# Causal attention with a gate, then eight routed experts, on one Trainium2 core: the start, the hand-over to the first expert and the last products put in another order, and one pair of batches fewer by one-hot products

## What is computed

```python
# x [16,128,256], ctx [16,128,256]; 8 experts, 512 slots each, token numbers drawn with repeats
x = x + xattn(layernorm(x), ctx)      # keys: rmsnorm(x) (causal) beside ctx, softmax, gate by sigmoid
...
h = layernorm(x).reshape(-1, 256)     # 2048 token rows
gathered = h[top_idx.T]               # [8, 512, 256]
g = gelu(gathered @ W1 + b1)          # [8, 512, 1024]
out_e = g @ W2 + b2
out = zeros.at[tok].add(out_e * combine_weights[tok, e])
return x + out
```

## Time and profile before

| | |
|---|---|
| median of 3 runs | 277.23 us (276.16 to 277.33) |
| the profiled execution: time | 277.63 us |
| the profiled execution: span from first to last instruction | 275.8 us |
| around the span | 1.8 us |
| mean granted TensorE clock | 0.991 |
| busy: PE, DVE, ACT, POOL | 265.7, 219.0, 188.2, 155.9 us |
| HBM read, written | 33.54 MB, 9.24 MB |

### The profile page before, as it was taken

The page is one execution under the profiler, slowest core; times in us unless marked ns, Lnnn a source line. Parts: engine busy times, 40 slices in busy tenths (PEclk is TensorE's granted clock), DMA queues, the critical chain, the costliest instruction groups (busy, mean ns, idle before and its releaser), DMA issues.

```text
span 275.8 us, 5127 instructions
## 1 busy us (share of the span) xinstructions
PE 265.7 (96%) x1474; PEld 226.7 (82%) x1474; DVE 219.0 (79%) x554; ACT 188.2 (68%) x349; POOL 155.9 (57%) x153
## 2 busy tenths in 40 slices
PE   6999999999989999999999999999999999999992
PEld 2688899999866888888888888888888888888992
DVE  1788999898986499968878896796887889689452
ACT  2488898887575976685677587658657758763540
POOL 4283865655843956556446466655645646605515
PEclk9799999999999999999999999999999999999998
DMA  7993247568454956455565544546555461201211
GB/s 219 358 263 94 77 123 218 155 214 276 114 182 123 350 160 157 124 192 167 138 195 163 154 139 135 157 122 209 156 138 189 156 175 53 67 26 47 62 38 69
DMA packets 30292, 42.44 MB, mean 154 GB/s; under 512 B 5251, under 2 KB 24015, under 8 KB 30148
## 3 DMA queue, kind: packets, MB, share of 16 engines
q1 hardware_dynamic: 25392, 30.00, 34.4%
q0 software_dynamic: 4608, 12.24, 15.4%
q10 hardware_dynamic: 276, 0.00, 0.1%
HBM read 33.54 MB, written 9.24 MB: 155 GB/s over the span
## 4 chain that ended last, share of the span: by engine, by line
PE 83%; DVE 6%; issue 4%; POOL 3%; ACT 2%; DMA 1%; DVEq 0%; POOLq 0%; ACTq 0%
PE bank L1398 19%; PE bank L1185 13%; PE bank L1186 12%; PE bank L1187 12%; PE bank L1399 10%; PE bank L1229 4%; PE bank L1274 3%; PE bank L1326 2%; PE bank L1345 1%; PE bank L1349 1%; PE bank L1346 1%; DMA x_all<-in_x_dram 1%; PE bank L1181 1%; POOL out_dram L552 1%; PE bank L1258 1%
## 5 line engine op out<-in xcount | busy, mean ns | idle before, releaser
L742 ACT ACTIVATE keysT<-bank,biasT 128x512 f32<-128x512 f32 x63 | 43.7, 693 | 55.6 <-PE bank L1187 41.8
L552 POOL DMA_INDIRECT out_dram<-h,sidx x32 | 36.8, 1151 | 41.9 <-DVE h L1077 37.0
L543 POOL DMA_INDIRECT x_all<-out_dram,idx_all x32 | 35.4, 1106 | 23.9 <-DMA out_dram<-h,sidx 16.5
L1185 PE MATMUL bank<-x_hi,w_parts 128*128 128x512 f32 (+1 forms) x114 | 45.1, 396 | 0.0
L1186 PE MATMUL bank<-x_lo,w_parts 128*128 128x512 f32 (+1 forms) x114 | 44.4, 389 | 0.0
L1187 PE MATMUL bank<-x_hi,w_parts 128*128 128x512 f32 (+1 forms) x114 | 44.1, 387 | 0.0
L1102 DVE TENSOR_TENSOR g_lo<-keysT,g_hi 128x512 fp32r<-128x512 f32 x32 | 22.1, 690 | 24.9 <-ACT g_hi L743 23.4
L1398 PE MATMUL bank<-w_parts,g_hi 128*128 128x512 f32 x112 | 40.5, 396 | 0.0
L539 POOL DMA_INDIRECT x_all<-token_rows,idx_all x28 | 29.0, 1036 | 19.4 <-DVE factor L1126 7.7
L1107 DVE TENSOR_TENSOR w_parts<-w_raw,w_parts 128x512 fp32r<-128x512 f32 x56 | 38.9, 696 | 0.0
L748 ACT CAST w_parts<-w_raw 128x512 fp32r<-128x512 f32 x56 | 34.9, 623 | 0.0
(11 more groups left out here) (186 smaller groups left out, 685.9 us busy)
## 6 DMA issues: line engine op xcount, KB each, us to landing
w_raw<-in_L_ffn_W_dram SPq DMA_DIRECT2D x32, 512.0 KB
idx_rows<-in_L_ffn_top_idx_dram SPq DMA_DIRECT2D x8, 256.0 KB, 4.0
out_dram<-x SPq DMA_DIRECT2D x8, 256.0 KB, 3.0
hn_cnat<-in_ctx_dram SPq DMA_DIRECT2D x7, 256.0 KB, 2.7
token_rows<-xn SPq DMA_DIRECT2D x7, 256.0 KB, 2.2
hn_cnat<-in_L_ffn_b_dram SPq DMA_DIRECT2D x1, 1024.0 KB, 6.9
x_all<-in_x_dram SPq DMA_DIRECT2D x3, 256.0 KB, 4.4
x_all<-in_x_dram SPq DMA_DIRECT2D x1, 768.0 KB, 8.1
```

What stands on the lines that cost most here:

```text
L543: g.indirect_dma_start(accg[:, t, :], None, flat, list_of(e, t)).then_inc(acc_in[t], 16)
L552: g.indirect_dma_start(flat, idx(sidx[:, t:t + 1].bitcast(U32), 0), newrow[:, t, :], None, bounds_check=N - 1, oob_is_err=False).then_inc( ...
L742: a.activation(g32[:, f % NG, :], ps_up[f % 2][:, :], ACT.Gelu_apprx_tanh, bias=bias)
L1185: t_.matmul(dst, lhs_hi, rhs_hi, start=first, stop=False)
```

## The change

It does six things. The start: k_w's load goes to ACT's queue as its first, gate_b is loaded by partition like norm_w, the product with the row of ones is replaced by four transposes of broadcast columns, both halves of M come before the transposes of pair 0, the context of pair 0 is transposed before the queries, one more warm-up product is made, and DVE takes the statistics of batches 6 to 9 later. The pairs: `EARLY_PAIRS` is NPAIR - 2, so that pair 5 is stored and gathered and only pairs 6 and 7 go by one-hot products; all gathers of expert 0's first rows move into pair 7. Pairs 6 and 7: DVE takes the statistics of x2 ahead of the gate, POOL the rstd of pair 5 ahead of the weight piece. The masks come ahead of expert 1's gathers. The end: `last_downs` takes four steps, and the last scatters' waits stand on their own instructions. Cut to its core:

```diff
@@ -51 @@
     NG = 4
-    EARLY_PAIRS = NPAIR - 3
+    EARLY_PAIRS = NPAIR - 2
@@ -359 @@
     load_weight(0, q_w, wts_in)
-    load_weight(1, k_w, wts_in)
@@ -390 @@
             load_ctx(r + 3)
-        if r == EARLY_PAIRS - 2:
+        if r == EARLY_PAIRS - 3:
...
                 sp.dma_start(rows_v[:, 2 * r + b, 0:H], xn_last[:, b, :]).then_inc(xn_out[r % 2], 16)
+            sp.wait_ge(onehot_rdy, NB - EARLY)
+            load_lists(IDX_PARTS - 1)
@@ -405 @@
                 sp.wait_ge(first_rows_in[t], 16)
-            for late in (LAST - 2, LAST - 1):
-                sp.wait_ge(xn_rdy, 2 * late + 2)
-                sp.dma_start(rows_v[:, 2 * late:2 * late + 2, 0:H], xn2[:, late % 2, :, :])\
-                    .then_inc(xn_out[late % 2], 16)
-            sp.wait_ge(onehot_rdy, NB - EARLY)
-            load_lists(IDX_PARTS - 1)
+            sp.wait_ge(xn_rdy, 2 * r + 2)
+            sp.dma_start(rows_v[:, 2 * r:2 * r + 2, 0:H], xn2[:, r % 2, :, :]).then_inc(xn_out[r % 2], 16)
@@ -500 @@
         if is_last(p):
-            gather_first_rows(range(1, NT))
+            gather_first_rows(range(1))
@@ -511 @@
         else:
-            if not is_last(p):
+            if not stats_first(p):
...
             rstd(p - 1, 1 - s)
-        if p == LAST - 1:
-            gather_first_rows(range(1))
+            if p == LAST - 1:
+                expert0_lo(p - 1)
+        if is_last(p):
+            gather_first_rows(range(1, NT))
@@ -548 @@
             pool.wait_ge(new_rdy, NT * e + t + 1)
-            take_waits(pool)
+            if not is_last(e):
+                take_waits(pool)
...
-    for s in range(2):
-        pool.wait_ge(xn_out[s], 16 * (NPAIR // 2) + 16 + 16 * s)
-        pool.wait_ge(x2_out[s], 16 * (NPAIR // 2) + 16)
-    gather_rows(1, 1)
...
                         pattern=[[1, C]], channel_multiplier=-NT).then_inc(seen_rdy, 1)
+    for s in range(2):
+        pool.wait_ge(xn_out[s], 16 * (NPAIR // 2) + 16 + 16 * s)
+        pool.wait_ge(x2_out[s], 16 * (NPAIR // 2) + 16)
+    gather_rows(1, 1)
@@ -583 @@
     a = nc.scalar
-    act.dma_start(norm_wT[:, :], norm_w.rearrange("(k p) -> p k", p=P), allow_slow_non_contiguous=True)\
+    act.dma_start(wts[:, 1, :, :], k_w.rearrange("(k p) h -> p k h", p=P)).then_inc(wts_in, 16)
+    act.dma_start(norm_wT, norm_w.rearrange("(k p) -> p k", p=P), allow_slow_non_contiguous=True)\
         .then_inc(nwT_in, 16)
-    act.dma_start(vec_rows[:, 0:H], norm_w.rearrange("(a h) -> a h", a=1)).then_inc(vec_in, 16)
-    act.dma_start(vec_rows[:, H:2 * H], gate_b.rearrange("(a h) -> a h", a=1)).then_inc(vec_in, 16)
+    act.dma_start(norm_w_gate_bT[:, 1, :], gate_b.rearrange("(k p) -> p k", p=P),
+                  allow_slow_non_contiguous=True).then_inc(gate_b_in, 16)
@@ -642 @@
     def attention(p, s, use):
-        if is_last(p):
-            act.wait_ge(xn_rdy, 2 * p - 2)
-            act.wait_ge(q_mm, NPAIR)
-            a.copy(late_hi[0], xn2[:, s, :, :]).then_inc(late_hi_rdy, 1)
@@ -655 @@
             hn_transposed(p + 2, s)
+        if is_last(p):
+            expert0_hi(p)
+            act.wait_ge(setup_mm, 4)
+            a.copy(biasT[:, :], banks[0][:, 0:NE * NF]).then_inc(setup_ev, 1)
@@ -674 @@
                 act.wait_ge(w_in[c], 16)
-        expert0_hi(p)
-        if is_last(p):
...
-            act.wait_ge(setup_mm, 4)
-            a.copy(biasT[:, :], banks[0][:, 0:NE * NF]).then_inc(setup_ev, 1)
-            a.activation(table_junk[:, :], junk[:, 0:2], ACT.Gelu_apprx_tanh)
+        if not is_last(p):
+            expert0_hi(p)
@@ -689 @@
             act.wait_ge(xn_rdy, 2 * p)
-            a.copy(late_hi[1], xn2[:, 1 - s, :, :]).then_inc(late_hi_rdy, 1)
+            a.copy(late_hi[0], xn2[:, 1 - s, :, :]).then_inc(late_hi_rdy, 1)
+            a.activation(table_junk[:, :], junk[:, 0:2], ACT.Gelu_apprx_tanh)
     M_high(0)
+    M_high(1)
     hn_transposed(0, 0)
-    M_high(1)
+    context_transposed(0, 0)
...
     query(0)
-    context_transposed(0, 0)
@@ -841 @@
     M_low(0)
+    M_low(1)
+    hnT_low(0, 0)
     x_sums(3, 4, 1)
-    hnT_low(0, 0)
     x_aggregates(2, 4)
-    M_low(1)
...
     x_rms(0, 4, 2)
-    x_stats(6, 10, 3)
-    x_variances(6, 10)
+    x_sums(6, 8, 3)
@@ -921 @@
         if not is_first(p):
-            if not is_last(p):
+            if not isinstance(p, int):
...
             residual(p - 1, 1 - s, last_use)
+            if stats_first(p):
+                stats2(p - 1, 1 - s)
+                aggr2(p - 1, 1 - s)
...
             v.tensor_copy(idx_f[:, :], idx_all[:, :, :].rearrange("p t e -> p (t e)")).then_inc(idx_rdy, 1)
+            x_sums(8, 10, 3)
@@ -947 @@
         if is_first(p):
+            x_aggregates(6, 10)
+            x_variances(6, 10)
...
             x_stats(10, NB, 4)
-        else:
+        elif not stats_first(p):
...
         else:
-            aggr2(p - 1, 1 - s)
+            if stats_first(p):
+                shift(p - 1, 1 - s)
+            else:
+                aggr2(p - 1, 1 - s)
...
         v.reciprocal(rinv[:, :], rsum[:, :]).then_inc(ri_rdy, 1)
-        if is_last(p):
-            dve.wait_ge(late_hi_rdy, 1)
-            dve.wait_ge(xn_rdy, 2 * LAST - 2)
-            v.tensor_tensor(late_lo[0], xn2[:, s, :, :], late_hi[0].bitcast(F32), ALU.subtract)\
-                .then_inc(late_lo_rdy, 1)
...
             dve.wait_ge(x_steps, steps[0])
-        elif not is_last(p):
+        elif not stats_first(p):
@@ -1015 @@
     last_pair_mixed(0)
-    shift(NPAIR - 2, 1 - last_s)
...
     last_pair_variance(1)
-    dve.wait_ge(late_hi_rdy, 2)
+    dve.wait_ge(late_hi_rdy, 1)
     dve.wait_ge(xn_rdy, 2 * LAST)
-    v.tensor_tensor(late_lo[1], xn2[:, 1 - last_s, :, :], late_hi[1].bitcast(F32), ALU.subtract)\
+    v.tensor_tensor(late_lo[0], xn2[:, 1 - last_s, :, :], late_hi[0].bitcast(F32), ALU.subtract)\
         .then_inc(late_lo_rdy, 1)
...
+    def last_pair_low(b):
+        dve.wait_ge(late_hi_rdy, 2 + b)
+        dve.wait_ge(last_xn[b], 1)
+        v.tensor_tensor(late_lo[1][:, b, :], xn_last[:, b, :], late_hi[1][:, b, :].bitcast(F32),
+                        ALU.subtract).then_inc(late_lo_rdy, 1)
...
+    last_pair_low(0)
...
                     ALU.mult, ALU.add).then_inc(last_xn[1], 1)
-    for b in range(2):
-        dve.wait_ge(late_hi_rdy, 3 + b)
-        dve.wait_ge(last_xn[b], 1)
-        v.tensor_tensor(late_lo[2][:, b, :], xn_last[:, b, :], late_hi[2][:, b, :].bitcast(F32),
-                        ALU.subtract).then_inc(late_lo_rdy, 1)
+    last_pair_low(1)
@@ -1160 @@
     pe.wait_ge(warm_rdy, 1)
-    keep_warm(9)
+    keep_warm(10)
@@ -1205 @@
     M_rows(0)
+    M_rows(1)
     hn_transposes(0, 0)
-    M_rows(1)
-    pe.wait_ge(vec_in, 32)
-    pe.wait_ge(ones_rdy, 1)
-    t_.matmul(banks[7][:, :], ones_row[:, :], vec_rows[:, :], start=True, stop=True).then_inc(bc_mm, 1)
+    context_transposes(0, 0, 0)
+    pe.wait_ge(nwT_in, 16)
+    pe.wait_ge(gate_b_in, 16)
+    for n in range(2):
+        for k in range(KH):
+            last = t_.transpose(banks[7][:, (n * KH + k) * P:(n * KH + k + 1) * P],
+                                norm_w_gate_bT[:, n, k:k + 1].broadcast_to([P, P]), ident[:, :])
+    last.then_inc(bc_mm, 1)
...
     query(0, 0)
-    context_transposes(0, 0, 0)
@@ -1248 @@
                 .then_inc(setup_mm, 1)
-            pe.wait_ge(log_rdy, 2 * NPAIR - 1)
-            pe.wait_ge(late_hi_rdy, 1)
-            for b in range(2):
-                late_rows(0, b, late_hi, first=b == 0)
@@ -1262 @@
         if is_last(p):
-            early_rows(range(1))
+            pe.wait_ge(log_rdy, 2 * NPAIR - 1)
+            for k in range(KH):
+                t_.matmul(ps_xT[k][:, :], junk[:, 0:P], junk[:, :], start=True, stop=False)
@@ -1291 @@
-    def late_rows(n, b, part, first=False):
+    def late_rows(n, b, part):
...
             t_.matmul(ps_xT[k][:, :], part[n][:, b, k * P:(k + 1) * P], onehot[:, 2 * n + b, :],
-                      start=first, stop=False)
+                      start=False, stop=False)
     each_pair(pe, attention)
-    early_rows(range(1, NT))
-    for n in range(2):
-        if n:
-            pe.wait_ge(late_hi_rdy, n + 1)
-            for b in range(2):
-                late_rows(n, b, late_hi)
-        pe.wait_ge(late_lo_rdy, n + 1)
+    early_rows(range(2))
+    pe.wait_ge(late_hi_rdy, 1)
+    for b in range(2):
+        late_rows(0, b, late_hi)
+    early_rows(range(2, 3))
+    pe.wait_ge(late_hi_rdy, 2)
+    late_rows(1, 0, late_hi)
+    pe.wait_ge(late_lo_rdy, 1)
+    for b in range(2):
+        late_rows(0, b, late_lo)
+    early_rows(range(3, NT))
+    for k in range(KH):
+        cols = slice(k * P, (k + 1) * P)
+        pe.wait_ge(late_hi_rdy, 3)
+        t_.matmul(ps_xT[k][:, :], late_hi[1][:, 1, cols], onehot[:, 3, :], start=False, stop=False)
         for b in range(2):
-            late_rows(n, b, late_lo)
-    for b in range(2):
-        pe.wait_ge(late_hi_rdy, 3 + b)
-        late_rows(2, b, late_hi)
-    for k in range(KH):
```

(9 more changed lines are left out.)

19 lines of the change are left out of this document (9 added, 10 removed).

## The result

| | before | after |
|---|---|---|
| median of 20 runs, us | 276.18 (276.0 to 277.41) | 277.34 (276.88 to 278.0) |
| profiled execution, us | 277.63 (the one forecast from) | 277.53 |
| its span, us | 275.8 | 275.7 |
| ratio after to before | | 1.0025, 95% interval 1.0014 to 1.0037 |

The change makes the kernel 0.25% slower, which is within the 0.5% that the forecast counted as no change; 274.9 us was forecast, 274.0 to 276.7 the range, and the time lies outside it. The runs of the kernel before fall into two groups, 12 of these 20 at 276.0 to 276.2 and 8 at 277.2 to 277.4; those of the changed kernel lie together, near the later group. The profiled execution that the forecast was made against, 277.63, is of the later group; so the medians lie 1.16 us apart, while the two profiled executions are 0.1 us apart.

The account below looks back on a forecast made before the run. PE was taken as full in the steady stages, waiting only at start, hand-over and end: 1.8 - 0.1 + 0.85 = 2.55 us off 277.63 gives 275.1, or 274.7 by the median; forecast 274.9, range 274.0 to 276.7.

Parts of the forecast that it names:

- The start: Up to pair 0's queries and first mask: reordered products and later statistics gain 1.8 us, from 1.0 to 2.3.
- I charge 0.2 for both: Pair 0: 0.2 us lost to DVE's returning statistics and POOL's later powers, which hold x_plus_h and pair 1's normed rows.
- The hand-over: Pairs 6 and 7 up to expert 0: 0.1 us lost, from 0.5 gained to 1.0 lost.
- the rstd wait: Last pair's first-half rstd behind POOL's gathers ends at 80.8 instead of 80.0; DVE mixes until 80.62, so 0.2 us shows.
- a rival at 0.10: Last pair: POOL's memset holds DVE's tensor_scalar, first product of expert 0 comes 0.85 us later, time 275.7; chance 0.10.
- Masks first: Memset and selects ahead of expert 1's gathers, which still land 2.7 us before PE wants them; nothing gained on PE.
- The clock rival: Waits after the last values product make PE's clock fall from 82 us, costing 1.3 us; time 276.1; chance 0.27.
- turn into waiting: Pairs 6 and 7: PE loses eight products, 1.9 us, but waits for gathers instead, reaching 84.9 us as before.
- The end: Last scatters: four steps per tile let the fourth scatter follow its own sum; 0.85 us gained, from 0.4 to 1.1.
- The rival of 0.15: Before the first queries: x lands 0.9 us later, or the clock falls, costing 0.8; time 275.7; chance 0.15.

Follow-up runs that it names:

- power earlier: The changed kernel with the last pair's first rstd on POOL ahead of the gather of tile 3; median 276.77 us, against 277.34.
- four repairs: Changed kernel with POOL's powers later, third context before lists, last pair's first rstd before tile 3's gather, masks held by a wait or last: 276.7 or 275.46 us.
- second trace: The kernel before, unchanged, profiled again in a run of 276.01 us; median of its eight runs 276.91 us.

## Why the prediction was wrong

**The start: right in its mechanism, wrong in what it is worth.** On the trace the first mask came 1.82 us earlier (2.0 forecast), the clock was full, x did not land later. Two steps failed. First, 1.8 was taken off a median; but the stretch at half clock which it removes is, by the two traces, there only in the executions of the later group, and against the early group the new order has 0.14 us. The two groups were in the three times shown (276.16 beside 277.23 and 277.33), and I called one trace "0.4 us above the median" rather than asking which group it was. Second, "I charge 0.2 for both" for what POOL's later powers hold up: it cost 0.65 on the trace, not through ACT's rows, as argued, but because POOL's normed rows now ran beside DVE's tensor_scalar.

**The hand-over: 0.1 forecast, 1.59 measured.** The forecast had the chain (store, gathers, rstd behind tile 3), and saw the rstd wait as costing 0.2, since DVE mixes until then. DVE mixed earlier than forecast, to 79.42, and shift followed at 79.97: power earlier gave 0.48. The greater part is the memset, 1.12, a rival at 0.10 with 0.85 us. The row of a tensor_scalar held by POOL's weight piece was the evidence, and I weighed it too low: two instructions of DVE stand there in a row on the path, the tensor_scalar behind the memset and the low part behind the select. By the Trainium skill (SBUF — State Buffer, SBUF: two separate sides), whichever of DVE and POOL starts first keeps the shared port for its whole instruction, if the DVE instruction runs in a mode with two ports or has two SBUF inputs (the latter only against a POOL instruction that reads SBUF). The rows of L1038 agree as far as they show it: the memset started at 81.86 and ended at 83.65, L1038 started at 82.13 and ended at 83.81; in which mode it ran, no row tells.

**Masks first: nothing gained, as forecast,** but not free.

**The clock rival** did not happen in this kernel's profiled execution, whose hand-over has a granted clock of 1.00. Three of its 20 runs have a mean clock of 0.990 or 0.991; if it fell at the hand-over there, it cost nothing that shows in the times, perhaps since DVE, held by the memset, was later than PE anyway. The fall is seen in the traces of both kernels with four repairs. That PE had room there was right; that the removed products "turn into waiting" was right too, and in those traces the clock fell behind such waits (1.25 us in one of them).

**The end: 0.85 forecast, 0.6 to 0.7 measured.** The mechanism is as forecast. PE's last products do not end where they did: between its last steps PE now starts two products 0.26 and 0.09 us later than the usual 0.12 us apart, where before had one such delay of 0.11, and the last sum starts 0.83 us later than before, of which the later start of expert 0 explains about half.

**The rival of 0.15** drew on the Trainium skill (TensorE: Matmul & The Clock Gate, Part 4: PE-mode transpose), by which transposes do not count as busy in the same way. Here the transposes ran ahead of the first queries and the clock stayed full in the trace; no run tells what they counted for.

## What to carry to other kernels

Before a forecast is made against one trace, look whether the times fall into groups, and find what differs; a stretch at half clock in the one trace may be a matter of chance, and its removal is then worth only its share of the executions. A small DVE instruction on the critical path can become as long as the POOL instruction that runs beside it, for some pairs and not for others: when a step of POOL is moved, write down what DVE does in its new place, and look in the traces for the same pair. And where PE waits between short runs of work, products of zeros in the wait can keep the clock: one of them here took away nearly all of a group of runs 1.2 to 1.5 us later, and the rest of a new order of the start added nothing to it; nine of them at the hand-over kept the clock and left the median.

## What the runs showed that I had not expected

- The granted clock fell in the shown trace of before and stayed full in its second trace, with the same instructions. Between the warm-up and pair 0's transposes PE stood 0.96 and 0.68 us in the first (the second stand is in the row below), 1.49 and 0.15 us in the second: 1.64 us in both. What decides is open.

```profile
7.72 1.05 PE L1181 MATMUL bank<-ident,hn_cnat 128*128 128x128 f32 x4 [0.68 <-DVE hn_cnat L811]
```

- A memset of POOL (1.79 us) held a DVE tensor_scalar of 128x256 for 1.68 us instead of 0.41; POOL's 128x512 product (1.28 us) held one of 128x6 for 0.82 instead of 0.16. POOL's powers on 128x4 to 128x12, up to 2.57 us long, held none that the traces show; in the changed kernel two tensor_scalars of L1038's shape take 0.73 us together, the second begun inside a power:

```profile
12.53 0.73 DVE L819 TENSOR_SCALAR h<-x_all,mv,pow_out 128x256 f32<-128x256 f32 x2
12.70 1.10 POOL L446 TENSOR_TENSOR pow_out<-pow_in,half_neg 128x4 f32<-128x4 f32 x1 [0.42 <-DVE pow_in L791]
```

- Nor did a memset hold every DVE instruction: before, beside that of the earlier trace rows, a subtraction of two SBUF tiles took 0.69 us, as elsewhere:

```profile
91.48 0.69 DVE L1102 TENSOR_TENSOR g_lo<-keysT,g_hi 128x512 fp32r<-128x512 f32 x1 [1.51 <-issue]
```

- The largest wait of PE between pair 1's and pair 2's logits (0.62 us for the third context) was worth 0.03 us: another wait ended with it.
